# Retention on one Trainium2 core: the next tile's projection crosses batches, rows are added in pairs, keys are scaled ahead of the state

## The reference, cut to what matters

```python
qkv = x @ W_qkv                                   # 16 heads of 16
ret = einsum('bhtd,bhsd->bhts', q, k) * decay     # gamma ** (t - s), causal
inner = einsum('bhts,bhsd->bhtd', ret, v)
cross = einsum('bhtd,hde->bhte', q, past_kv) * 256
y = inner + cross
yn = (y - mean) * rsqrt(var + EPS) * gn_weight + gn_bias   # mean and var over a whole batch
x = layernorm(x + yn)
```

## Time and profile before

| | |
|---|---|
| median of 3 runs | 1036.89 us (1036.85 to 1037.99) |
| profiled execution | 1033.99 us, of which its span is 1032.3 us |
| PE / DVE / ACT / POOL busy, share of the span | 83% / 67% / 45% / 25% |
| mean granted TensorE clock | 0.919 of full speed |
| retention | from 0 to the last normalised rows of x, at 291.27 us; the first matmul of the next stage starts at 291.99 us |

### The profile page before, as it was taken

The page is one execution under the profiler, slowest core; times in us unless marked ns, Lnnn a source line. Parts: engine busy times, 40 slices in busy tenths (PEclk is TensorE's granted clock), DMA queues, the critical chain, the costliest instruction groups (busy, mean ns, idle before and its releaser), DMA issues. The chain is left out here.

```text
span 1032.3 us, 21811 instructions
## 1 busy us (share of the span) xinstructions
PE 857.2 (83%) x8084; PEld 675.5 (65%) x8084; DVE 687.0 (67%) x1502; ACT 462.5 (45%) x953; POOL 262.5 (25%) x331
## 2 busy tenths in 40 slices
PE   6888888898769999993998789989978838999950
PEld 5766776777557777772443378777656728999950
DVE  2476667667645777776798934678787884646438
ACT  2433333343357777771883434544533212444410
POOL 1246445222110132212000000004232023656323
PEclk9999999999969999996999989999988858999985
DMA  8400000000000000000357744434212301646437
GB/s 299 148 12 21 15 15 11 19 21 0 0 1 1 2 1 1 1 1 1 91 127 174 177 95 114 121 89 172 82 59 73 115 18 30 206 115 206 104 77 265
DMA packets 73094, 79.45 MB, mean 77 GB/s; under 512 B 22336, under 2 KB 66240, under 8 KB 71616
## 3 DMA queue, kind: packets, MB, share of 16 engines
q1 hardware_dynamic: 68048, 72.36, 23.3%
q0 software_dynamic: 3968, 5.25, 3.1%
q10 hardware_dynamic: 1008, 0.91, 0.3%
HBM read 50.71 MB, written 27.79 MB: 76 GB/s over the span
## 5 line engine op out<-in xcount | busy, mean ns | idle before, releaser
L698 DVE TENSOR_TENSOR r_prob<-r_pS,const 128x512 f32<-128x512 f32 x128 | 79.5, 684 | 39.2 <-PE r_pS L525 39.2
L1029 DVE SCALAR_TENSOR_TENSOR f_gl<-f_g,small_first,f_gh 128x512 fp32r<-128x512 f32 x64 | 47.3, 747 | 40.8 <-ACT f_gh L967 38.5
L1264 PE MATMUL q_pE<-q_xT,att_res 128*128 128x512 f32 x128 | 60.8, 631 | 6.8 <-ACT q_xT L1204 6.8
L908 PE MATMUL f_pY<-wpjT,f_gh 128*128 128x256 f32 x256 | 65.1, 289 | 0.0
L909 PE MATMUL f_pY<-wpjT,f_gl 128*128 128x256 f32 x256 | 62.7, 279 | 0.0
L908 PEld LDWEIGHTS f_pY<-wpjT,f_gh 128*128 128x128 f32 x256 | 48.1, 188 | 15.2 <-issue 13.4
L2190 POOL DMA_INDIRECT sum_dram<-e_yo,y_id x24 | 39.1, 1629 | 70.5 <-ACT e_yo L2279 62.3
L815 POOL TENSOR_SCALAR t_ey<-t_es 128x8 f32<-128x8 f32 x4 | 1.0, 249 | 216.0 <-ACT t_sqrow L1738 216.0
L961 ACT ACTIVATE f_g<-f_pH 128x512 f32<-128x512 f32 x64 | 38.0, 594 | 39.0 <-PE f_pH L897 38.2
L897 PE MATMUL f_pH<-f_xh,wfcT 128*128 128x512 f32 x128 | 53.0, 414 | 1.4 <-DVE f_xl L1023 1.4
L2309 DVE SCALAR_TENSOR_TENSOR e_hl<-e_pH,e_hh 128x320 fp32r<-128x320 f32 x64 | 27.7, 484 | 39.0 <-ACT e_hh L2272 38.9
(11 more groups left out here) (291 smaller groups left out, 2464.8 us busy)
## 6 DMA issues: line engine op xcount, KB each, us to landing
kv_dram<-att_res SPq DMA_DIRECT2D x16, 512.0 KB, 4.3
t_ring<-kv_dram SPq DMA_DIRECT2D x128, 64.0 KB, 2.3
wi<-L_ffn_wi SPq DMA_DIRECT2D x8, 1024.0 KB
wo<-L_ffn_wo SPq DMA_DIRECT2D x8, 1024.0 KB
x_res<-L_attn_x SPq DMA_DIRECT2D x8, 512.0 KB, 5.1
q_dram<-att_res SPq DMA_DIRECT2D x8, 512.0 KB, 3.0
t_q<-q_dram SPq DMA_DIRECT2D x64, 64.0 KB, 2.9
x_dram<-x_res SPq DMA_DIRECT2D x8, 512.0 KB, 3.0
```

Source lines behind the costliest of these rows:

```text
L698: dve.tensor_tensor(prob[t % 2][:, r, :, :], pS[r][:, :, :], dec[:, r, :, :], ALU.mult)\
L908: pe.matmul(out, gh[c % 4][:, cols], net.wpjT[:, c, :], start=(c == 0 and t % 2 == 0), stop=False, skip_group_check=True)
L1029: dve.scalar_tensor_tensor(out=gl[c % 4][:, :], in0=g[c][:, :], scalar=net.lnw[:, c:c + 1], in1=gh[c % 4][:, :], op0=ALU.mult, op1=ALU.sub ...
L1264: mm = pe.matmul(out[:, :], net.wqkvT[:, k, n * P:(n + 1) * P], xT[p][:, k, :], start=(k == 0), stop=(k == KD - 1))
```

## The change

PE, ACT and DVE now take `project(0, 0)` and its copies ahead of the batches. In slot 3 of every batch but the last, `project(b + 1, 0)` and the two `take` stand where there was none; nothing stands at the top of a batch any more. To leave room for the last batch, which has no successor, the loops run over batches 1 to 6, and batch 7 is written in line. DVE runs `keys` ahead of `carry`. It adds both tiles of a pair (`add_rows`), then takes the statistics of both (`measure_rows`, split off from `add_rows`), and runs all four `norm_rows` of a batch at its end. For the batch behind the last one the order of rows stays as it was, with `measure_rows` behind each `add_rows`. Left out are `turn_keys` and `keys` of tile 3, the whole v of tile 3 on ACT, and `decay_queries` of tile 0 on POOL. In batch 0 ACT sums the magnitudes of both feed-forward weights in slots 1 and 2 (two halves each) and not in slots 1, 2 and 3; the transfer of the second tile of x goes out ahead of the table `const`.

```diff
         def decay_queries(b, t):
+            if t == 0:
+                return
             i = b * TPB + t
...
             for odd, half in enumerate((vE, vO)):
-                nc.scalar.activation(half[t][:, :].rearrange("p (g two e) -> p g two e", two=2, e=HD)[:, :, odd, :],
-                                     heads[:, :, odd, :], ACT.Copy)
-            nc.scalar.activation(v[t][:, :], pV, ACT.Copy).then_inc(qv_taken.sem, 1)
+                ins = nc.scalar.activation(half[t][:, :].rearrange("p (g two e) -> p g two e", two=2, e=HD)[:, :, odd, :],
+                                           heads[:, :, odd, :], ACT.Copy)
+            if t < TPB - 1:
+                ins = nc.scalar.activation(v[t][:, :], pV, ACT.Copy)
+            ins.then_inc(qv_taken.sem, 1)
...
-        def batch(b, before):
-            take(b, 0)
+        def batch(b, before, behind):
             for t in range(TPB):
                 if t + 1 < TPB:
                     take(b, t + 1)
+                elif behind:
+                    take(b + 1, 0)
                 if t == 1 and before:
                     normed(b - 1)
                 if t:
                     result(b, t - 1)
                 elif before:
                     result(b - 1, TPB - 1)
-                if not before and t:
-                    for half in ((), (0,), (1,), (0, 1))[t]:
-                        magnitudes(1 if t == 3 else 0, half)
+                if not before and t in (1, 2):
+                    for half in range(2):
+                        magnitudes(t - 1, half)
...
         act.dma_start(net.small0[:, :], a["small0"]).then_inc(small0_in.sem, 16)
+        act.dma_start(xT[1][:, :, :], a["xT"][1]).then_inc(x_in[1].sem, 16)
         act.dma_start(net.const[:, :], a["consts"][:, 0:KEPT]).then_inc(c_in.sem, 16)
-        for t in range(1, TPB):
+        for t in range(2, TPB):
             act.dma_start(xT[t][:, :, :], a["xT"][t]).then_inc(x_in[t].sem, 16)
         act.dma_start(net.small[:, :], a["small"]).then_inc(small_in.sem, 16)
         act.wait_ge(c0_in.sem, c0_in.after(16))
         act.wait_ge(cleared.sem, cleared.after(1))
         act.wait_ge(zeroed.sem, zeroed.after(1))
-        batch(0, False)
-        with act.Fori(1, BATCH) as b:
-            batch(b, True)
+        take(0, 0)
+        batch(0, False, True)
+        with act.Fori(1, BATCH - 1) as b:
+            batch(b, True, True)
+        batch(BATCH - 1, True, False)
...
             if not first:
                 pe.wait_ge(k_taken.sem, k_taken.after(i))
-                pe.wait_ge(ks_ready.sem, ks_ready.after(i if t == 0 else i - 1)) if (t != 1 or not isinstance(b, int)) else None
+                turned = b * (TPB - 1) + max(t - 1, 0)
+                if not isinstance(turned, int) or turned:
+                    pe.wait_ge(ks_ready.sem, ks_ready.after(turned))
...
-        def batch(b, before):
-            project(b, 0)
+        def batch(b, before, behind):
             for t in range(TPB):
                 if t + 1 < TPB:
                     project(b, t + 1)
+                elif behind:
+                    project(b + 1, 0)
                 if t == 1 and before:
...
-                turn_keys(b, t)
+                if t < TPB - 1:
+                    turn_keys(b, t)
                 if t >= 2 and before:
                     for j in (2 * t - 4, 2 * t - 3):
                         turn_back(b - 1, j, 4 * (b * TPB + t) + 1 + j % 2)
 
-        batch(0, False)
+        project(0, 0)
+        batch(0, False, True)
         mean_magnitudes()
-        with pe.Fori(1, BATCH) as b:
-            batch(b, True)
+        with pe.Fori(1, BATCH - 1) as b:
+            batch(b, True, True)
+        batch(BATCH - 1, True, False)
...
+
+        def measure_rows(b, t):
+            i = b * TPB + t
             dve.wait_ge(back_taken.sem, back_taken.after(i + 1))
             dve.bn_stats(bst[:, t, :], y1[t][:, :]).then_inc(steps.sem, 1)
             dve.wait_ge(steps.sem, steps.done(1))
...
-        def batch(b, before):
-            take(b, 0)
+        def batch(b, before, behind):
             for t in range(TPB):
                 if t + 1 < TPB:
                     take(b, t + 1)
+                elif behind:
+                    take(b + 1, 0)
                 if t == 1 and before:
                     group_var(b - 1)
                 decay(b, t)
                 if t == 1 and before:
                     group_affine(b - 1)
+                if t < TPB - 1:
+                    keys(b, t)
                 if t:
                     carry(b, t - 1)
-                keys(b, t)
                 if t >= 2 and before:
-                    for j in (2 * t - 4, 2 * t - 3):
+                    pair = (2 * t - 4, 2 * t - 3)
+                    for j in pair:
                         add_rows(b - 1, j)
-                        if j:
-                            norm_rows(b - 1, j - 1)
+                    for j in pair:
+                        measure_rows(b - 1, j)
             if before:
-                norm_rows(b - 1, TPB - 1)
+                for j in range(TPB):
+                    norm_rows(b - 1, j)
 
         norm_parts()
-        batch(0, False)
+        take(0, 0)
+        batch(0, False, True)
         mean_of_halves()
-        with dve.Fori(1, BATCH) as b:
+        with dve.Fori(1, BATCH - 1) as b:
             steps.enter(b - 1, 2 + 3 + 2 + 4)
-            batch(b, True)
-            steps.leave(BATCH - 1)
+            batch(b, True, True)
+            steps.leave(BATCH - 2)
+        batch(BATCH - 1, True, False)
         group_var(BATCH - 1)
         group_affine(BATCH - 1)
         for t in range(TPB):
             add_rows(BATCH - 1, t)
+            measure_rows(BATCH - 1, t)
             if t:
                 norm_rows(BATCH - 1, t - 1)
         norm_rows(BATCH - 1, TPB - 1)
```

17 lines of the change are left out of this document (8 added, 9 removed).

## The result

The changed kernel takes 1004.6 us, median of four runs (1001.63 to 1008.75), against 1036.87 for the kernel before in the same session. The ratio is 0.9701, 95% interval 0.9681 to 0.9720: faster, by 32 us. The forecast was 1009.8, range 1001 to 1020. The profiled execution lasts 1002.86, its span 1001.2, mean granted clock 0.925.

What follows compares the result with a forecast made beforehand. PE, its matmuls plus its waits, was taken as the bound. Gains 24.5 - 1.4 + 2.2 + 1.8 = 27.1 off the profiled 1033.99 give 1006.9, plus 2.9 to the median: 1009.8 us, range 1001 to 1020.

Steps and rivals of the forecast that it cites:

- Bound and waits: Whole kernel: PE, busy 83% of the span, is the engine to follow; its time is matmuls plus its own waits.
- Slot 2 to slot 3: Each batch but the last: projection adds 2.87, waits for state (0.87) and rows (1.29) go; 6.78 becomes 7.15 us.
- Slot 3 to slot 0: Between batches: one projection and two transposes fewer, waits for v and the keys' copy gone; 6.9 instead of 11.84 us.
- Slot 0 to slot 1: DVE's slot 3 work delays the copy of tile 1's keys; 5.95 becomes 6.25 or 6.65 us, plus 0.7 for powers.
- the powers' price: End of slot 3: DVE norms wait for POOL's one-element powers under a shared-port lock; 0.7 us per batch.
- Rival 1: No lock on the powers: DVE's four norms run freely, 4.6 us less, 1005; chance 0.2.
- Slot 1 to slot 2: No gain: 7.61 us stays, 8.6 in batches 1 to 4; the wait for `r_rT` grows from 0.23 to 0.5.
- Clock: Batches 2 to 7: clock stays at 1.00 once slot 3's pair of waits is gone; 3 to 4.5 us of the gain.
- Rival 2: Clock falls all the same behind new waits in slots 0 to 2, 1.5 us per batch, 9 more, 1019; chance 0.2.
- Start and end: Batch 0 loses waits and transposes, 2.2 us; batch 7's norm begins 14.75 instead of 16.54 behind slot 2's scores, 1.8 less.
- Rival 4: Waits of 0.87 and 1.29 partly reappear in slot 3; half of both in six batches, 6.5 more, 1016; chance 0.1.
- Rival 3: Slower: DVE's end of batch becomes the bound, PE stalls at `turn_keys` of slot 0 and stays cold; chance 0.03.

Runs made afterwards that it cites:

- e9: The changed kernel with DVE scaling tile 1's keys ahead of `group_affine` too; one profiled run, 1003.8 us.
- e6: The changed kernel with POOL's scaling of tile 1's queries in batches 5 to 7 held until DVE has copied tile 1's keys; 1006.16 us.
- e8: The changed kernel with a test in front: eight DVE norms per phase beside POOL idle, one-element powers, or products 1 to 256 wide; 1017.4 us.

## Why the prediction was right, and where its size was off

**Bound and waits.** Right. The waits read in the earlier trace rows were what could be had. The gain was forecast at 27.1 and is 31.1 between the two profiled executions (1033.99 and 1002.86). The 4.0 too little are 1.7 in slots 0 to 1 and 1.3 in slots 2 to 3 of the sum, 0.3 in batch 7, 0.9 at the start and 0.5 at the end, less 0.6 that the rest of the program gives back. The median was put 2.9 above the profiled execution and lies 1.7 above it, so that 1009.8 stands against 1004.6.

**Slot 2 to slot 3.** Forecast 7.15, measured 6.93. State and rows are covered as said. The 0.22 is in the price of the projection. It was taken from two groups that start behind a wait, and the first matmuls of such a group take 0.11 longer: from the projection's first row to its next one it is 1.00 at 244.81 and 0.89 at 241.08. In a row without waits, as between batches 6 and 7 of the changed kernel, a projection takes 2.65 (215.40 to 218.05) and not 2.87. Six batches of it are 1.3 us.

**Slot 3 to slot 0.** Forecast 6.9, measured 6.88 to 6.92 in five batches and 6.71 in the sixth. That the five fit is luck: the projection is 0.22 too dear in this sum too, and the gap at the turn of the loop with its restart, which the forecast does not have, costs 0.2.

**Slot 0 to slot 1.** A wait moved in, as forecast, on the engine, at the place and behind the operations that were named. Forecast, with the powers' price, 6.95 in batches 2 to 4 and 7.35 later; measured 6.69 and 6.93. The step that failed is the price of 0.7 us per batch for norms beside powers: "I take 0.7, since the nearest row shows a full block". The nearest row was one of 256 elements and the case one of a single element. Measured: 0 (three norms in 1.02, and 2.68 against 2.67 in the test). Nor does that row show a full block. The prediction reads in the earlier trace rows that the norm ends its own length behind POOL's operation; that one ends at 80.47 and the norm at 80.63, 0.16 behind, so that it lost 0.43.

Part of the 0.7 was made up by two things not counted. POOL makes the powers one after the other, the statistics of two tiles now come 0.69 apart, and what POOL does for a tile takes 0.8, so the last power comes about 0.2 later and takes 0.1 longer: the fourth norm waits 0.44 where 0.11 was left for it. And in batches 2 to 4 that norm takes 0.58 and not 0.38.

**Rival 1** (no lock on the powers, 1005, chance 0.2) names what happened on the powers. Its number is met in part by luck: by its sum slot 0 to 1 would be 6.25 and 6.65, less than the 6.69 and 6.93 measured, and slots 2 to 3 and the start make up for that.

**Slot 1 to slot 2.** Right: 7.61 and 8.6 stay, the wait for `r_rT` grew to 0.55, and e9 shows the chain that holds it.

**Clock.** Right in the profile, the clock is 1.00 in batches 1 to 7. Rival 2 was not void, though: in e6 slow stretches stand behind waits of 0.97 and 0.65 in batches with quantising, and in e9 behind one of 2.34. They are an occasional price and likely a part of the scatter of the four runs: these take 1001.63, 1002.86, 1006.34 and 1008.75 at mean granted clocks of 0.926, 0.925, 0.923 and 0.920. Where the stretches of the three others lie is not known, since one execution was traced. Rival 2's price of 1.5 a batch is what e6 shows (1.55). The forecast's "3 to 4.5 us of clock" in the loop before was too much, however: from scores to scores the three slow batches there are 0.95, 0.95 and 0.78 longer, 2.7 in all.

**Start and end.** Forecast 2.2 and 1.8. The scores of batch 1 come 3.07 earlier, though the projection ahead of them runs at the lower clock for a while in both profiled executions; where the 0.9 more comes from was not taken apart. The norm of batch 7 begins 14.26 behind the scores of slot 2 (247.99 - 233.73, the latter from the PE timeline) instead of 16.54, so 2.3.

**Rival 4**, waits that reappear in slot 3, did not happen: the timeline has no wait there. **Rival 3** came nowhere near: slot 0 to 1 is longer than before by 1.0 us a batch in the sum, and by 1.2 in batch 7.

## What to carry to other kernels

In a pipeline over slots, count each engine's work slot by slot and not over the loop: PE had two projections in one slot and none in another, and four of its six waits stood there, at the top of a batch and in slot 3. When a stall is filled, ask which queue is now the longest in front of the next hand-over; here it was DVE's, and moving work that nobody waits for (four norms) out of that slot was worth a further 10 us (median 994.46 against 1004.6, measured at different times but with ratios to before of 0.9607 and 0.9701; 7.1 of it in the sum). When two neighbouring rows could price an unknown, take the one that is like the case in what does the blocking (elements), not in what is easiest to see (an operation beside another). And take the price of a piece of work from a place where it runs as it will run: behind a wait, a projection read 0.22 dearer than in a row.

## What the runs showed of the hardware

- A POOL operation on one element can run 0.66 us without holding up DVE at all. Four of 64 elements cost eight norms 0.1 us together, four of 256 elements 2.0 (e8).
- A norm beside POOL's `tensor_scalar` 256 wide of 1.15 us takes 0.58 and is over first; beside POOL's `tensor_tensor` of 0.73 it takes 0.82. Operations of DVE on 128x2 elements are held as well, 0.77 and 0.64 where 0.40 and 0.16 stand in another kernel.
- The granted clock can fall in one execution and not in another behind the same waits of the same schedule, here 0.97 and 0.65 us in batches 2 to 4 of e6_queries_later and of the changed kernel, for 1.55 us a batch.
- PE's first weight load behind the turn of its loop comes 0.15 to 0.18 late at four turns of the changed kernel, and the first matmuls of a group behind a wait take 0.11 longer than those in a row.
